# The passage from the first attention to the second in a two-layer transformer kernel: keys and values move to the score banks, ScalarE normalises the last tiles, and one list orders all engines

## What is computed

```python
# layer 0: attention (8 heads of 8), then a gated mixture feed-forward; x1 = x + gate * (out @ Wo_w.T + Wo_b)
# the second attention starts from the normalised x1:
q = (x @ Wq.T).reshape(b, s, H, HD)        # H = 32 heads of 128, here s = 1024 tokens
k = (x @ Wk.T).reshape(b, s, HKV, HD)      # HKV = 8 groups
v = (x @ Wv.T).reshape(b, s, HKV, HD)
q = _rmsnorm(q, q_norm_w)
k = _rmsnorm(k, k_norm_w)
scores = einsum(qg, k) / sqrt(HD) + bias   # causal, with a slope per head
out = einsum(softmax(scores), v) @ Wo.T
# layer 1 ends with a feed-forward with dequantised weights
```

## Time and profile before

| | us |
|---|---|
| median of 3 runs (1472.74 to 1473.64) | 1472.75 |
| the profiled execution | 1472.16 |
| its span in the trace | 1470.4 |
| PE busy | 1379.7 (94%) |
| VectorE busy | 986.7 (67%) |
| ScalarE busy | 855.6 (58%) |
| GpSimd busy | 634.0 (43%) |

### The profile page before, as it was taken

One profiled execution on the slowest core, in us unless ns is written; L12 is line 12 of the kernel. 1 busy time (PEld: TensorE's weight loads), 2 busy tenths in 40 slices (PEclk: granted clock), 3 DMA queues, 4 the chain that ended last, 5 costly groups with the idle time before them and its releaser, 6 DMA issues.

```text
span 1470.4 us, 21362 instructions
## 1 busy us (share of the span) xinstructions
PE 1379.7 (94%) x7350; PEld 1082.0 (74%) x7350; DVE 986.7 (67%) x1852; ACT 855.6 (58%) x2105; POOL 634.0 (43%) x965
## 2 busy tenths in 40 slices
PE   4989987899999999999999999999999999989997
PEld 3733435688778888877888887888878877768786
DVE  6666656577677777678777777777687777675233
ACT  2335572566666666676666666676666666563211
POOL 4313263644344545445443555444444445433311
PEclk9979998999999999999999999999999999999999
DMA  4200022101020111002010101100020111113010
GB/s 141 65 1 1 1 77 77 37 8 45 15 73 21 40 35 39 30 30 73 1 60 13 61 21 39 59 15 31 30 73 1 45 35 38 37 58 134 15 58 29
DMA packets 35883, 61.02 MB, mean 41 GB/s; under 512 B 9056, under 2 KB 13280, under 8 KB 35776
## 3 DMA queue, kind: packets, MB, share of 16 engines
q1 hardware_dynamic: 35776, 59.66, 12.7%
HBM read 49.68 MB, written 9.96 MB: 41 GB/s over the span
## 4 chain that ended last, share of the span: by engine, by line
PE 66%; DVE 8%; issue 6%; ACT 1%; POOL 1%; DMA 0%; POOLq 0%; SPq 0%; DVEq 0%
PE T L2246 7%; PE T L1877 7%; PE T L1879 6%; PE T L1878 6%; PE S L1879 4%; PE S L1878 4%; PE S L1877 4%; PE VB L1879 4%; PE VB L1877 4%; PE WB L1877 4%; PE WB L1879 4%; PE WB L1878 4%; PE VB L1878 4%; PE T L2139 2%; DVE R L1654 2%
## 5 line engine op out<-in xcount | busy, mean ns | idle before, releaser
L852 POOL TENSOR_TENSOR RI<-SM,C 128x1 f32<-128x1 f32 x256 | 143.3, 560 | 503.2 <-ACT PB L1187 501.9
L1647 DVE CUSTOM_DVE_ANT_0 PB<-S,REL,SLC 128x128 f32<-128x128 f32 (+7 forms) x256 | 204.5, 813 | 78.3 <-PE S L1879 76.8
L1187 ACT ACTIVATE PB<-PB,NM 128x128 f32<-128x128 f32 (+7 forms) x256 | 198.8, 777 | 69.6 <-DVE NM L1647 64.7
L1251 ACT ACTIVATE R<-T 128x512 fp32r<-128x512 f32 x288 | 170.6, 593 | 100.5 <-PE T L2246 98.6
L853 POOL TENSOR_SCALAR PB<-PB,RI 128x128 f32<-128x128 f32 (+7 forms) x256 | 215.2, 840 | 25.2
L1654 DVE TENSOR_TENSOR R<-T,R 128x512 fp32r<-128x512 f32 x288 | 197.5, 688 | 42.1 <-ACT R L1251 23.7
L2246 PE MATMUL T<-C,PB 128*128 128x128 f32 x1152 | 176.6, 276 | 12.0 <-DVE R L1654 6.8
L2246 PEld LDWEIGHTS T<-C,PB 128*128 128x128 f32 x1152 | 134.1, 140 | 48.1 <-DVE R L1654 18.0
L1166 ACT ACTIVATE JUNK<-WB 128x128 bf16<-128x128 f32 x256 | 67.2, 277 | 92.8 <-PE WB L1879 92.8
L1877 PE MATMUL WB<-R,XT 128*128 128x512 f32 x288 | 116.6, 405 | 2.7 <-ACT G L1144 2.7
L1878 PE MATMUL WB<-R,XT 128*128 128x512 f32 x288 | 113.8, 395 | 0.0
(11 more groups left out here) (277 smaller groups left out, 3496.6 us busy)
## 6 DMA issues: line engine op xcount, KB each, us to landing
RAW<-w SPq DMA_DIRECT2D x86, 256.0 KB, 2.8
DQ<-codes SPq DMA_DIRECT2D x16, 352.0 KB, 3.5
DQ<-absmax SPq DMA_DIRECT2D x16, 352.0 KB, 3.0
dequantised<-DQ SPq DMA_DIRECT2D x16, 352.0 KB, 2.2
PB<-x SPq DMA_DIRECT2D x12, 256.0 KB, 3.3
PB<-dequantised SPq DMA_DIRECT2D x5, 512.0 KB, 4.7
PB<-x_scratch SPq DMA_DIRECT2D x8, 256.0 KB, 3.9
out<-PB SPq DMA_DIRECT2D x8, 256.0 KB, 2.0
```

The source lines that it names most:

```text
L852: ch.link(e.tensor_tensor(RI[:, k:k + 1], SM[:, k:k + 1], C[:, C_EXP + 5:C_EXP + 6], ALU.pow))
L1187: e.activation(pb(m, a, 0, L), pb(m, a, 0, L), ACT.Exp, scale=-1.0, bias=NM[:, k:k + 1], accum_out=SM[:, k:k + 1]).then_inc(exp_done, 1)
L1251: e.activation(r(PT + AT[i, ("PV", kb)] % 3 * 1024, 512), T[AT[known, it] % 2][:, :], ACT.Copy).then_inc(t_act, 1)
L1647: e.tensor_tensor_reduce(out=pb(m, a, 0, L), in0=bank[:, 0:L], in1=REL[:, TOK - L:TOK], scale=SLC[:, a:a + 1], scalar=3.0e38, op0=ALU.add, ...
```

## The change

The tail's order becomes one list written out by hand, 64 items long, which all engines follow. With it:

1. **Keys and values in the score banks.** `KV` b is projected into S0 or S1 (bank b mod 2, half b mod 4 / 2), so four may be open, and it no longer takes a turn in the ring of T0 and T1, which has 23 items now. The release is a new count, `kv_free`: one for the low half of the values (a new item `VL`) and one for the scaled keys (`SC`). VectorE no longer copies the keys to SBUF: `SC` scales them straight from PSUM.
2. **The first query projection in VB**, no longer in WB, which leaves WB to `WO` and `PQ` 1.
3. **ScalarE normalises tiles 4 to 7**: one `Identity` with bias -mean * rstd and scale rstd (`apply_act`). GpSimd makes the bias with two more small instructions for each tile (`rstd(t, True)`).
4. **Order.** `PQ` 0 moves from the front of the tail to behind `WO` 7; the key tiles 0 to 3 come sooner; `S0` stands before `KT` 7 and `SQ` 1.

The diff, cut to its core:

```diff
-KV_STEP = (0, 0, 1, 2, 6, 7, 8, 10)
-SC_STEP = (1, 1, 2, 3, 7, 8, 9, 11)
-KT_STEP = (2, 3, 4, 5, 8, 9, 10, 11)
...
+TAIL = [("XT", EARLY - 1), ("KV", 0), ("OS", 4), ("KV", 1), ("VL", 0), ("OH", 4), ("OS", 5), ("KV", 2), ("VL", 1), ("WO", 4),
+        ("OH", 5), ("OS", 6), ("KV", 3), ("SC", 0), ("LS", 4), ("WO", 5), ("OH", 6), ("OS", 7), ("VL", 2),
+        ("SC", 1), ("KT", 0), ("LA", 4), ("LS", 5), ("WO", 6), ("OH", 7), ("SC", 2), ("KT", 1), ("XT", 4),
+        ("LA", 5), ("LS", 6), ("WO", 7), ("PQ", 0), ("VL", 3), ("SC", 3), ("KT", 2), ("XT", 5), ("LA", 6),
+        ("LS", 7), ("KV", 4), ("KT", 3), ("XT", 6), ("VL", 4), ("SQ", 0), ("LA", 7), ("KV", 5), ("SC", 4),
+        ("QT", 0), ("XT", 7), ("VL", 5), ("KT", 4), ("KV", 6), ("SC", 5), ("PQ", 1), ("KT", 5), ("KV", 7),
+        ("VL", 6), ("SC", 6), ("KT", 6), ("S0", 0), ("VL", 7), ("SC", 7), ("KT", 7), ("SQ", 1), ("QT", 1)]
...
+def kv_bank(b):
+
+    return b % 2, b % 4 // 2 * 512
...
+                if bias:
+
+                    ch.link(root)
+                    ch.link(e.tensor_tensor(NB[:, k:k + 1], MV[:, k, 0:1], RSTD[:, k:k + 1], ALU.mult))
+                    root = e.tensor_scalar(NB[:, k:k + 1], NB[:, k:k + 1], -1.0, 0.0, ALU.mult, ALU.add)
...
+                e.activation(X1N[t], X1[t], ACT.Identity, bias=NB[:, k:k + 1], scale=RSTD[:, k:k + 1]).then_inc(xn_ready, 1)
...
-                ch.done(e.tensor_copy(KN[b % 4], T[k % 2][:, 0:HD]))
-                e.tensor_tensor(kv(0, 3 * TOK + b * P, P), T[k % 2][:, HD:2 * HD], kvf(0, 2 * TOK + b * P, P),
-                                ALU.subtract).then_inc(t_free, 1)
...
-                e.tensor_scalar(KN[b % 4], KN[b % 4], SQK[:, 2, b:b + 1], None, ALU.mult).then_inc(k0_ready, 1)
+                e.tensor_scalar(KN[b % 4], kv_psum(b, 0, HD), SQK[:, 2, b:b + 1], None, ALU.mult).then_inc(kv_free, 1)
...
+                if kind == "PQ" and b == 0:
+                    pe.wait_ge(sums_ready, UNITS)
+                    project_q(block_of(b), None, lambda kt: C_PRO["Q", 0, kt], VB, q0_full)
...
+                    if b >= 4:
+                        pe.wait_ge(kv_free, max(KV_FREE["VL", b - 4], KV_FREE["SC", b - 4]) + 1)
...
+                        if b:
+                            pe.wait_ge(kv_free, 2 * NT)
```

More of the change, by code:

```diff
@@ L604, in y_psum, with kv_psum @@
             return S[a // 2][:, a % 2 * D:(a % 2 + 1) * D]
+        def kv_psum(b, lo, hi):
+            k, o = kv_bank(b)
+            return S[k][:, o + lo:o + hi]
         def tile(block):
@@ L961, in _ @@
                         rstd(NT + it[1])
[L962 to L971, removed]
+            for kind, t in TAIL:
+                if kind == "WO":
+                    add_x(t)
+                elif kind == "LS":
+                    rstd(NT + t, True)
+                elif kind == "KV":
+                    inverse_k(t)
+                elif kind == "PQ":
+                    inverse_rms(0, t, 4 * t + 4, 4)
             w1_low("K", 1, 0)
@@ L1217, in _ @@
                         w1_high("K", 1, 0)
                         w1_high("K", 1, 1)
+                elif kind == "KT":
+                    high_k(0, b, T_AT[x] + 1, T[T_AT[x] % 2])
+                elif kind == "QT":
+                    high_q(b, T_AT[x] + 1, T[T_AT[x] % 2])
+                elif kind == "S0":
+                    for a in range(4):
+                        exp1(0, a, P, a + 1)
             def lines(g, i, part):
@@ L1618, in copy_k, with scale_qk @@
                 e.tensor_copy(QN[:, 4 * HD:5 * HD], tk[:, 0:HD]).then_inc(t_free, 1)
-            def scale_qk(m, icount, tcopy):
+            def scale_qk(m, icount, tcopy, bank=WB, free=w_free):
                 dve.wait_ge(inv_ready, icount)
@@ L1711, in _ @@
                         bias_max(0, a, P, S_PRO + a + 1, S[a % 2])
-            dve.wait_ge(t_free, T_BASE)
+            dve.wait_ge(kv_free, 2 * NT)
             dve.sem_inc(v_split, NT)
@@ L2115, in ring0, with project_q @@
                     pe.wait_ge(m_free, M_END)
-            def project_q(row, wait_w, chunk):
-                pe.wait_ge(w_free, wait_w)
+            def project_q(row, wait_w, chunk, bank=WB, full=w_full):
+                if wait_w is not None:
+                    pe.wait_ge(w_free, wait_w)
                 for kt in range(KT):
@@ L2122, in project_q, with project_kv @@
                     c = kt * 768
-                    last = mm3(WB[:, :], xt(0, kt, row * P, P), xt(1, kt, row * P, P), r(W_H + c, 512),
+                    last = mm3(bank[:, :], xt(0, kt, row * P, P), xt(1, kt, row * P, P), r(W_H + c, 512),
                                r(W_L + c, 512), kt == 0, kt == KT - 1)
-                last.then_inc(w_full, 1)
-            def project_kv(row, k, bank, chunk):
-                ring(k)
+                last.then_inc(full, 1)
+            def project_kv(row, k, bank, chunk, full=t_full):
+                if k is not None:
+                    ring(k)
                 pe.wait_ge(split, chunk + (QL1 + 1))
@@ L2133, in project_kv @@
                                r(W_L + c, 256), kt == 0, kt == KT - 1)
-                last.then_inc(t_full, 1)
+                last.then_inc(full, 1)
             def transpose_q(k, bank):
```

144 lines of the change are left out of this document (71 added, 73 removed).

## The result

The changed kernel takes 1469.06 us (median of nine, 1465.52 to 1470.55) against 1473.32 (median of nine, 1468.53 to 1474.0) for the kernel before, run beside it: 0.9972 of the time, 95% interval 0.9963 to 0.998. That is 4.3 us less, where the forecast was 8.3. The profiled execution took 1470.25 (span 1468.5), 1.9 us less than the profiled one of before.

What follows compares the result with a forecast made beforehand. PE's waits and half clock in the tail bound the kernel; the chain falls from 53.4 to 41.7 us, 11.7 less, and one clock fall costs 3.4: 1472.16 - 8.3 = 1463.9, or 1464.5 against the median, range 1460.5 to 1470.

Steps and rivals of the forecast that it cites:

- The walk: Tail: new engine lists timed item by item from profile rows, ending slot 0's first projection at 262.05, good to about 1 us.
- A to G: Seven consecutive stretches of the tail's last-ending chain, key projections to slot 0's projection: 41.7 us against 53.4 at full clock.
- The 1.28 us of the earlier trace: Key scaling from SBUF beside GpSimd's subtraction; from PSUM, SC 7 was expected at 0.29, otherwise 1.0 us is added.
- the prediction's sum, which said the opposite: Tail normalisation: ScalarE preferred despite 0.78 against VectorE's 0.71, since PE waits for VectorE; frees 4 x 0.7 us of its queue.
- One fall of the clock: Likeliest case: one half-clock stretch in the tail, most likely the last place, costing 3.4 us; gain 8.3, chance 0.50.
- two thin places: Tail stretches with little PE work: 229.4 to 234.2 (1.7 us in 4.8) and 252.6 to 259.3 (some 2 in 6.7).
- Both falls: Case: the clock falls at both thin places of the tail; projection ends at 268.9, gain 4.8, chance 0.20.
- The gap of 2.18 us before 283.48: Slot 0, behind the tail: this gap, with full work around it, brought no clock fall in the old trace.
- From there on the same picture as before, shifted: Expected sign: after slot 0's projection starts at 259 to 264, the trace repeats the old one, only shifted.
- Given back: Case: an unseen wait in the order, or half clock from 231 us through slot 0's projection; gain 0.7, chance 0.08.
- slower: Case: the clock stays down until after slot 0's scores, making the kernel 4.5 us slower; chance 0.04.
- three signs of being wrong: PE waiting over 3 us before XT 4, a new wait in slot 0, or the clock down past slot 0's projection.

Runs made afterwards that it cites:

- e6: Changed kernel with its items back in the old kernel's order, keys and values still in the score banks: 1465.2 us.
- e5: Kernel before the change plus 38 throwaway matmuls ahead of TensorE's waits in the tail: 1469.11 us.
- e4: Changed kernel with VectorE instead of ScalarE normalising tiles 4 to 7, and no GpSimd bias: 1467.93 us.
- e10: Changed kernel plus 24 throwaway matmuls at the start of the first attention, tail unedited: 1462.79 us.
- e3: Changed kernel plus throwaway matmuls only at the end of the tail (KT 6, third score, KT 7, QT 1): 1466.51 us.
- e2: Changed kernel plus throwaway matmuls only at the first thin place (3 ahead of KT 0, 8 ahead of XT 4): 1462.63 us.
- e8: Changed kernel with the first query projection, PQ 0, moved ahead of XT 4: 1464.8 us.
- e9: Changed kernel plus eight throwaway matmuls ahead of slot 0's transposes that wait 2.18 us: 1466.13 us.
- e12: e11 plus e10's throwaway matmuls in the first attention: 1456.23 us, 0.9874 to 0.9899 of the kernel before.
- e1: Changed kernel plus 32 throwaway matmuls in all thin places of the passage: 1463.59 us.
- e11: e8's list plus 24 throwaway matmuls in the passage and e9's eight in slot 0: 1460.42 us.

## Why the forecast was wrong, step by step

*The walk* was right. Its sum at full clock, A to G, is 41.7 us; with the clock held the trace gives 41.92. `XT` 4 was put at 234.2 from a start of 220.33, and stands at 235.49 from a start of 221.66, 13.8 us on against 13.9. The gaps at the end were forecast as 0.8, 1.2, 1.1 and 1.6 and are 0.80, 0.88, 0.92 and 1.54. ScalarE's 0.82, GpSimd's 0.55 a tile, and `SC` 7's 0.34 are within 0.05 us of their terms. But in this trace `SC` 7 does not fall under the subtraction (two of them, 2.49 us together), as the walk had it: it starts at 261.69, just after 259.16 + 2.49 = 261.65.

```profile
261.69 0.34 DVE L1689 TENSOR_SCALAR L0S<-S,SQK 128x128 f32<-128x128 f32 x1
```

```profile
259.16 2.49 POOL L949 TENSOR_TENSOR R<-RAW,R 128x512 fp32r<-128x512 f32 x2
```

So the changed kernel's own trace doesn't test that term; others do. In e6 `SC` 7 starts at 258.70, 0.13 us into the subtractions that start at 258.57, and takes 0.35; in e5, with its input in SBUF as before, it starts 0.07 us into them and takes 1.30. The 1.28 us of the earlier trace rows did not come back with the input in PSUM. On that point the rule of the Trainium skill that the prediction cites (SBUF — State Buffer, Who interferes with whom) agrees with the traces. The Trainium skill's rule for kernel authors (ScalarE: Activation LUTs, Rules for kernel authors) that products and sums belong on VectorE could be tested only as the whole step: 0.82 against 0.71 us for one. The medians show no difference, and the nearest pair of traces, e4 and e10, has VectorE 0.5 us ahead, too little to decide between the rule and the prediction's sum, which said the opposite.

*The term that failed is the clock: "One fall of the clock ... 3.4", chance 0.50.* There were three falls in the passage, and they cost 6.4 us, not 3.4. The price of the last place was right: 3.4 by e3. What was wrong is that only it was counted: the two early falls cost another 3.0 together, where the forecast had 3.4 for the first place alone. I had allowed two thin places, because the kernel before had two falls; the third fall (249 us) came behind a gap of 1.22 us that follows one of 0.84, which I had not taken for a thin place. That the new list makes more falls because it spreads the waiting over shorter gaps is not shown: the same gaps had no fall behind them in e10's and e2's traces. "Both falls", 268.9 from a start of 220.33, is 48.6 us long, which is the length measured (48.3): in length that rival came true, but by luck: three falls made it and not two, and e10's trace of the same list has two falls and takes 46.1.

*"The gap of 2.18 us before 283.48 ... brought none"* took one trace's luck for a rule. Six of eleven traces have a fall there, the changed kernel's among them: 1.6 us that the sum lacked. "From there on the same picture as before, shifted" fell with it.

*What lies ahead of the passage* was taken as equal. It starts between 217.5 and 221.7 us in the twelve traces of kernels that are the same up to there, and the start goes with the time at half clock ahead of it: 217.5 us with 14 us of it (e4, e8), 219.0 to 220.4 with 20 or 21 (eight traces), 221.5 and 221.7 with 24 (e9 and the changed kernel); e10 and e12 start at 216.1 and 215.9 with 3. Of the shortfall in the profiled executions, 8.3 - 1.9 = 6.4 us, 3.2 are the passage, 1.6 the slots, 1.3 this start and 0.3 the rest; the medians, over nine runs each, give 4.3 us of gain rather than 1.9, so part of this is the chance of one execution.

*The rivals.* "Given back" and "slower" did not happen; the clock came back at the last of the twelve matmuls of slot 0's projection, near 269.7, where before it came back halfway through. The range held the time. None of the three signs of being wrong that the forecast named showed, though it was off by half: they looked for a longer wait or a clock that stays down, and not for more falls.

*Open.* Why a gap is followed by a fall in one trace and not in another isn't settled: the slot's gap is the same 2.18 us in e1 (with a fall) and e8 (without), and the pair of 0.84 and 1.22 us has one behind it in the changed kernel and none in e10. e2 lost the slot's fall without an edit there. The Trainium skill (TensorE: Matmul & The Clock Gate, The HAM clock gate) says that the matmul at which the clock rises differs between runs of one kernel. The traces agree that the places differ, for the falls too: the twelve without e10's throwaways reach the first key projection up to 4.1 us apart with the same code ahead of it.

## What to carry to other kernels

Where TensorE runs at the lower clock behind short waits, price the dependencies and the clock apart: hold the clock with throwaway matmuls into a free bank ahead of the waits, and what is left is the chain. A change that shortens waits and spreads them may pay in dependencies (here 6.9 us) and show less in the time, because the clock still falls (6.4 us of the passage in one trace, 4.2 in another with the same list); one trace shows neither where the clock falls nor that it doesn't. Before a trace is held against another, note the falls of both. Look for the half clock over the whole span first: the cheapest 3.3 us of this kernel lay in a stretch that the change never touched.

## What the chip showed that I had not expected

- No gap between 81 and 89 us is longer than 1.38 us, and the clock is at 0.50 behind them; with 24 matmuls in these gaps it stays at 1.00.
- Throwaways cost nothing that shows where TensorE waits: 32 of them in e1's passage left it 0.2 us from the walk without them.
- In e1, e9 and e11 the clock also fell between 1287 and 1321 us, once in e1 and twice in the other two, where the other eleven traces kept it, and the rest of the span is 1167.8 to 1168.2 us instead of 1165.5 to 1166.5: there, too, falls come in some executions and not in others.
